# Cross-attention and mixture-of-experts kernel: the router's threshold search with one of its three counts on ScalarE, selection and slot positions rewritten, bf16 one-hots for the slots

## The reference

```python
T = B * S                                  # 2048 tokens
cap = max(1, T // E)                       # 256
probs = jax.nn.softmax(xt @ Wg, axis=-1)
pT = probs.T
_, top_idx = jax.lax.top_k(pT, cap)        # each expert takes its 256 likeliest tokens
sel = jnp.zeros((E, T), dtype=bool).at[jnp.arange(E)[:, None], top_idx].set(True)
masked = jnp.where(sel, pT, -jnp.inf)
assigned = sel.any(axis=0)
tok2exp = jnp.where(assigned, jnp.argmax(masked, axis=0), jnp.argmax(pT, axis=0))
...
h = jax.nn.gelu(xt @ W1[e], approximate=False) @ W2[e]     # weighted by the chosen probability
```

## Time and profile before

| | |
|---|---|
| device time, median of 3 | 428.44 us (428.04 to 429.25) |
| the profiled execution | 426.05 us, its span 424.2 us |
| busy: PE, ACT, DVE, POOL | 359.4, 259.4, 208.5, 118.9 us |
| router, from the last logits to the first index fetched by POOL | 279.5 to 326.6 us |
| mean granted TensorE clock | 0.93 of full speed |

### The profile page before, as it was taken

The page is one execution under the profiler, slowest core; times in us unless marked ns, Lnnn a source line. Parts: engine busy times, 40 slices in busy tenths (PEclk is TensorE's granted clock), DMA queues, the critical chain, the costliest instruction groups (busy, mean ns, idle before and its releaser), DMA issues.

```text
span 424.2 us, 10996 instructions
## 1 busy us (share of the span) xinstructions
PE 359.4 (85%) x4207; PEld 232.5 (55%) x4208; DVE 208.5 (49%) x785; ACT 259.4 (61%) x354; POOL 118.9 (28%) x175
## 2 busy tenths in 40 slices
PE   2989898999999999999999999841139799989893
PEld 1646456445343545453435468830039788879782
DVE  5849973745373646363646558358877010101010
ACT  1456456899999999999999925430000444444430
POOL 4244789300030303030302100000001345555543
PEclk9999999899999999999999999555559999999999
DMA  8325995304494446434842352800000322222210
GB/s 271 97 102 154 275 272 167 125 4 101 112 258 113 105 117 201 118 98 126 235 122 39 94 182 96 287 15 1 0 2 2 93 64 76 65 81 68 76 50 26
DMA packets 36760, 47.61 MB, mean 112 GB/s; under 512 B 8460, under 2 KB 25794, under 8 KB 36705
## 3 DMA queue, kind: packets, MB, share of 16 engines
q1 hardware_dynamic: 33808, 40.26, 33.2%
q0 software_dynamic: 2560, 6.30, 5.0%
q10 hardware_dynamic: 337, 0.32, 0.2%
HBM read 32.71 MB, written 13.81 MB: 110 GB/s over the span
## 4 chain that ended last, share of the span: by engine, by line
PE 63%; DVE 13%; ACT 9%; DMA 6%; issue 5%; SPq 2%; POOL 1%; POOLq 0%; ACTq 0%; DVEq 0%
PE ps L1002 15%; PE ps L981 14%; PE ps L966 7%; PE ps L1204 7%; PE ps L1194 7%; ACT pbuf L790 6%; PE ps L950 4%; DVE v_st L1581 3%; PE ps L1091 2%; PE ps L1065 2%; DMA pbuf<-in_L_xattn_Wkv 2%; DMA mid<-token_rows,take_ix 2%; DMA sums<-mid 2%; PE ps L1082 1%; SPq L491 1%
## 5 line engine op out<-in xcount | busy, mean ns | idle before, releaser
L790 ACT ACTIVATE pbuf<-ps 128x1024 f32<-128x1024 f32 (+3 forms) x192 | 169.3, 1030 | 3.6 <-PE ps L981 3.5
L1454 DVE SCALAR_TENSOR_TENSOR pbuf<-pbuf,seen 128x128 f32<-128x128 f32 (+2 forms) x288 | 79.2, 317 | 64.1 <-ACT pbuf L790 63.6
L981 PE MATMUL ps<-q_st,k_st 98*32 98x512 bf16 (+4 forms) x2048 | 102.5, 320 | 3.1 <-ACT pbuf L790 2.6
L1002 PE MATMUL ps<-pbuf,v_st 128*32 128x512 f32 (+4 forms) x1024 | 97.8, 477 | 1.0 <-DVE pbuf L1454 0.9
L981 PEld LDWEIGHTS ps<-q_st,k_st 98*32 98x32 bf16 x2048 | 52.5, 96 | 69.8 <-ACT pbuf L790 27.1
L667 POOL TENSOR_TENSOR mid<-mid 64x1024 f32<-64x1024 f32 x7 | 16.6, 2370 | 126.7 <-DMA mid<-reciprocals 109.3
L867 ACT COPY piece_f<-wts 128x1024 f32 x20 | 20.9, 1045 | 48.8 <-DVE more L1669 45.0
L1682 DVE SCALAR_TENSOR_TENSOR mid<-ps,slot_gate,mid 128x256 f32<-128x256 f32 x20 | 9.7, 484 | 81.9 <-PE ps L1204 81.9
L1204 PE MATMUL ps<-wts,mid 128*128 x160 | 39.0, 387 | 4.9 <-ACT mid L877 3.2
L1002 PEld LDWEIGHTS ps<-pbuf,v_st 128*32 128x32 f32 x1024 | 27.5, 110 | 25.7 <-issue 11.8
L1194 PE MATMUL ps<-mid,piece_f 128*128 128x128 f32 x320 | 39.1, 275 | 1.2 <-ACT mid L872 0.7
(11 more groups left out here) (215 smaller groups left out, 387.2 us busy)
## 6 DMA issues: line engine op xcount, KB each, us to landing
wts<-in_L_ffn_W SPq DMA_DIRECT2D x16, 512.0 KB, 4.9
k_st<-k_cut SPq DMA_DIRECT2D x48, 147.2 KB, 3.0
q_st<-q_cut SPq DMA_DIRECT2D x48, 128.0 KB, 2.9
q_cut<-wts SPq DMA_DIRECT2D x8, 384.0 KB, 3.6
k_cut<-wts SPq DMA_DIRECT2D x8, 384.0 KB, 4.2
xres<-in_x SPq DMA_DIRECT2D x4, 512.0 KB, 7.1
token_rows<-xres SPq DMA_DIRECT2D x4, 512.0 KB, 4.5
mid<-mid SPq DMA_DIRECT2D x28, 64.0 KB, 2.6
```

The costliest lines, as they stand in the source:

```text
L790: nc.scalar.activation(pbuf[:, s % 2, r, c0:c1], st_ps[(s * GH + r) % NST][:, c0:c1], ACT.Exp, scale=SCALE).then_inc(exp_done, 1)
L981: last = nc.tensor.matmul(st_ps[(s * GH + r) % NST][c:c + 32, a:z], k_st[pa][:, r, t * P + c:t * P + c + 32], q_st[pa][:, r, q0 + a - c0:q ...
L1002: last = nc.tensor.matmul(o_ps[32 * r:32 * r + 32, a:z], v_st[pa][:, t, r, :], pbuf[:, s % 2, r, a + dc:z + dc], start=(t == 0), stop=(t = ...
L1454: last = nc.vector.scalar_tensor_tensor(a, a, 3.0e38, seen[:, off:off + w], ALU.min, ALU.mult)
```

## The change

- **Keys.** They are fp32 in steps of 2 to the 15th, read by DVE straight from PSUM; the softmax is halved and stored expert-major. The second half's key comes from one instruction instead of four.
- **Rounds.** DVE makes two compares, ACT the third as `Sign(cand - key)` with a sum. PE adds a constant (a matmul that waits for nobody) and two products, one by `same_e` for DVE's counts, one by `same_h` (minus a half) for ACT's. `nxt` is now waited for.
- **Selection.** Sign, an equality, a scan, one combined order and one comparison; the way back is a bf16 matmul by `ident_2`. A bitwise or marks the held probability, a max-scan finds the peak, an equality makes the indicator `r_ind`.
- **Positions.** Offsets are made by matmuls (`same_s`, `prev_s`, `unbefore`, `lower_e`) and by adding a large constant that rounds to whole tiles.
- **Slots.** One-hots and operands are bf16. Token index first (32 matmuls), then the tiles' experts, then the weight in three bf16 parts (16 matmuls of 72 columns). The ring is gone. `keep_running` is 20, 40 and 20 in place of 80 and 90.
- Constants: `expert_constants` shrinks from 11 instructions to 1; `count_constants` (6 new) runs on DVE in the second group of heads.

```diff
@@ tensor
             for i in range(ROUNDS):
 
+                at = bank(1 + i % 2)[:, 0:3]
+                nc.tensor.matmul(at, ones_b[:, :], offset_b[:, 0:3], start=True, stop=False, skip_group_check=True)
                 pe.wait_ge(cnt_done, i + 1)
-                nc.tensor.matmul(bank(1)[:, 0:3], same_e[:, :], cnt_b[:, 0:3], start=True, stop=True).then_inc(tot_ready, 1)
+                nc.tensor.matmul(at[:, 0:2], same_e[:, :], cnt_d[:, 0:2], start=False, stop=True, skip_group_check=True)
+                pe.wait_ge(acnt_done, i + 1)
+                nc.tensor.matmul(at[:, 2:3], same_h[:, :], cnt_a[:, 0:1], start=False, stop=True,
+                                 skip_group_check=True).then_inc(tot_ready, 1)
...
-            keep_running(80)
...
+            keep_running(20)
+            pe.wait_ge(tile_v_done, 1)
             for t in range(TT):
                 pe.wait_ge(tile_made, t + 1)
-                last = nc.tensor.matmul(bank(3)[:, 0:2 * NS], in_tile[t % RING], hv[:, t, :, :].rearrange("p c n -> p (c n)"),
-                                        start=(t == 0), stop=(t == TT - 1)).then_inc(slots_ready, 1)
-
+                if t == 0:
+                    pe.wait_ge(row_v_done, 1)
+                nc.tensor.matmul(bank(3)[:, 0:NS], in_tile[t], tile_v[:, t, :], start=(t == 0), stop=False, skip_group_check=True)
+                last = nc.tensor.matmul(bank(3)[:, 0:NS], in_tile[t], row_v[:, t, :], start=False, stop=(t == TT - 1),
+                                        skip_group_check=True)
+            last.then_inc(slots_ready, 1)
+            keep_running(40)
+            pe.wait_ge(gate_v_done, 1)
+            for t in range(TT):
+                last = nc.tensor.matmul(bank(5)[:, 0:3 * NS], in_tile[t], gate_v[:, t, :, :].rearrange("p c n -> p (c n)"),
+                                        start=(t == 0), stop=(t == TT - 1))
+            last.then_inc(gates_ready, 1)
...
-            keep_running(90)
+            keep_running(20)
@@ scalar
-            nc.scalar.activation(warm[:, 3:4], ones_b[0:1, 0:1], ACT.Gelu)
+            nc.scalar.activation(warm[:, 3:4], ones_b[0:1, 0:1], ACT.Sign)
+
+            def compare(i):
+
+                act.wait_ge(cand_made, i + 1)
+                c = start_c[:, 0, :] if i == 0 else start_c[:, 1, :] if i == len(SHIFTS[0]) else cand
+                nc.scalar.activation(r_side, r_key[0 if i < len(SHIFTS[0]) else 1], ACT.Sign, scale=-1.0, bias=c[:, 3:4],
+                                     accum_out=cnt_a[:, 0:1]).then_inc(acnt_done, 1)
...
+            nc.scalar.activation(warm[:, 4:5], ones_b[0:1, 0:1], ACT.Gelu)
+            act.wait_ge(of_tile_done, 1)
+            nc.scalar.activation(row_v, of_tile, ACT.Identity, scale=frow[:, 0:1]).then_inc(row_v_done, 1)
@@ vector
-                    seq(nc.vector.scalar_tensor_tensor(r_eq, r_key[0], cand[:, 0:1], r_low, ALU.is_equal, ALU.mult))
-                    seq(nc.vector.tensor_scalar(r_sel, r_key[0], cand[:, 0:1], float((1 << LOW) + 1), ALU.is_gt, ALU.mult))
-                    seq(nc.vector.tensor_tensor(r_key[1], r_sel, r_eq, ALU.add))
-                    seq(nc.vector.tensor_scalar(cand[:, :], digit[:, i, :], 1.0, None, ALU.add))
-                for n, sh in enumerate(shifts):
-                    for j in range(1, 4):
-                        last = nc.vector.tensor_scalar(r_ge[j - 1], r_key[half], cand[:, j:j + 1], 0.0, ALU.is_ge, ALU.add,
-                                                       accum_out=cnt_b[:, j - 1:j])
+                    nc.vector.scalar_tensor_tensor(r_key[1], r_key[0], cand[:, 0:1], r_low, ALU.subtract, ALU.add).then_inc(cand_made, 1)
+                    v.wait_ge(cand_made, i + 1)
+                for n, w in enumerate(STEPS_OF[half]):
+                    for j in range(1, 3):
+                        last = nc.vector.tensor_scalar(r_junk[j], r_key[half], c[:, j:j + 1], 0.0, ALU.is_ge, ALU.add,
+                                                       accum_out=cnt_d[:, j - 1:j])
                     last.then_inc(cnt_done, 1)
...
+            nc.vector.tensor_scalar(r_eq, r_key[1], thr, 0.0, ALU.is_equal, ALU.add, accum_out=eq_n[:, 0:1]).then_inc(cnt_done, 1)
+            seq(nc.vector.tensor_tensor_scan(r_scan, r_one, r_eq, 0.0, ALU.mult, ALU.add))
+            v.wait_ge(acnt_done, ROUNDS + 1)
+            seq(nc.vector.scalar_tensor_tensor(r_order, r_side, APART, r_scan, ALU.mult, ALU.add))
...
+            nc.vector.tensor_scalar(r_sel, r_order, bank(5)[:, 0:1], float(CAP), ALU.add, ALU.is_le).then_inc(sel_done, 1)
...
+            seq(nc.vector.tensor_tensor(held3.bitcast(I32), bank(6)[:, 0:P].rearrange("p (e t) -> p t e", e=E).bitcast(I32), pr.bitcast(I32),
+                                        ALU.bitwise_or))
+            seq(nc.vector.tensor_tensor_scan(r_peak, r_keep, r_held, 0.0, ALU.mult, ALU.max))
+            nc.vector.tensor_tensor(r_ind3[:, 1:, :].rearrange("p e t -> p t e"), peak3,
+                                    peak3[:, :, E - 1:E].broadcast_to([P, TT, E]), ALU.is_equal).then_inc(ind_done, 1)
+            v.wait_ge(ind_done, 1)
+            seq(nc.vector.tensor_tensor(r_hot, r_ind[:, TT:], r_ind[:, 0:TE], ALU.subtract))
+            v.wait_ge(tot_there, 1)
+            nc.vector.tensor_copy(r_tot, bank(2)[:, 0:P]).then_inc(tot_done, 1)
+            v.wait_ge(tot_done, 1)
+            seq(nc.vector.tensor_scalar(r_gint, peak3[:, :, E - 1].bitcast(I32), (1 << 30) - 1, None, ALU.bitwise_and))
+            v.wait_ge(n_ready, 1)
+
+            seq(nc.vector.tensor_scalar(r_base, bank(0)[:, 0:1], P / 2 - 0.5, TO_TILES, ALU.add, ALU.add))
+            nc.vector.tensor_scalar(r_size, zeros_b[:, :], r_base, TO_TILES, ALU.add, ALU.subtract).then_inc(size_done, 1)
+            v.wait_ge(size_done, 1)
+            seq(nc.vector.tensor_scalar(r_nt, bank(0)[:, E:2 * E], P / 2 - 0.5, TO_TILES, ALU.add, ALU.add))
             v.wait_ge(rank_ready, 1)
+            seq(nc.vector.tensor_tensor(r_tmp, bank(1)[:, 0:TE], r_hot, ALU.mult))
+            seq(nc.vector.reduce_sum(r_pos, t3, AX.X))
+            seq(nc.vector.tensor_scalar(r_up, r_pos, -(P / 2 - 0.5), TO_TILES, ALU.add, ALU.add))
+            nc.vector.tensor_tensor(of_tile, r_up[:, :, None].broadcast_to([P, TT, NS]), r_mark[:, None, :].broadcast_to([P, TT, NS]),
+                                    ALU.is_equal).then_inc(of_tile_done, 1)
+            seq(nc.vector.scalar_tensor_tensor(r_lo, r_up, TO_TILES, r_pos, ALU.subtract, ALU.subtract))
+            v.wait_ge(of_tile_done, 1)
+            nc.vector.tensor_tensor(tile_v, of_tile, r_tilev[:, :, None].broadcast_to([P, TT, NS]), ALU.mult).then_inc(tile_v_done, 1)
+            for t in range(TT):
+                nc.vector.tensor_scalar(in_tile[t], fcol_n, r_lo[:, t:t + 1], None, ALU.is_equal).then_inc(tile_made, 1)
+
+            seq(nc.vector.tensor_scalar(r_nt, r_nt, TO_TILES, 1.0 / P, ALU.subtract, ALU.mult))
             seq(nc.vector.tensor_tensor_scan(r_end, r_one[:, 0:E], r_nt, 0.0, ALU.mult, ALU.add))
...
+            v.wait_ge(slots_ready, 1)
+            nc.vector.tensor_scalar(slot_tok[:, :], bank(3)[:, 0:NS], float(T), None, ALU.add).then_inc(idx_done, 1)
...
+            nc.vector.tensor_tensor(gate_v, of_tile[:, :, None, :].broadcast_to([P, TT, 3, NS]),
+                                    r_gs[:, :, :, None].broadcast_to([P, TT, 3, NS]), ALU.mult).then_inc(gate_v_done, 1)
...
```

More of the change, by code:

```diff
@@ L675, in _ @@
                 scale(g)
[L676 removed]
+            pool.wait_ge(idx_done, 1)
             pool.wait_ge(rows_sent, 16 * 2 * (TT // 4))
@@ L858, in _ @@
             act.sem_inc(fg_done, 2)
-            nc.scalar.activation(warm[:, 3:4], ones_b[0:1, 0:1], ACT.Gelu)
+            nc.scalar.activation(warm[:, 3:4], ones_b[0:1, 0:1], ACT.Sign)
[4 more added lines that the diff above has]
+                                     accum_out=cnt_a[:, 0:1]).then_inc(acnt_done, 1)
+            with nc.allow_low_precision(reason="counts of at most 128"):
+                for i in range(ROUNDS):
+                    compare(i)
+                act.wait_ge(cand_made, ROUNDS + 1)
+                nc.scalar.activation(r_side, r_key[1], ACT.Sign, scale=-1.0, bias=cand[:, 0:1],
+                                     accum_out=lt_n[:, 0:1]).then_inc(acnt_done, 1)
+            nc.scalar.activation(warm[:, 4:5], ones_b[0:1, 0:1], ACT.Gelu)
+            act.wait_ge(of_tile_done, 1)
+            nc.scalar.activation(row_v, of_tile, ACT.Identity, scale=frow[:, 0:1]).then_inc(row_v_done, 1)
             act.wait_ge(texp_done, 2)
@@ L1164, in _ @@
-            nc.tensor.matmul(bank(2)[:, 0:1], prev_e[:, :], cnt_b[:, 1:2], start=True, stop=True).then_inc(tot_ready, 1)
+            nc.tensor.matmul(at, same_h[:, :], eq_n[:, 0:1], start=False, stop=False, skip_group_check=True)
+            nc.tensor.matmul(at, prev_e[:, :], eq_n[:, 0:1], start=False, stop=True, skip_group_check=True).then_inc(tot_ready, 1)
             pe.wait_ge(sel_done, 1)
```

(31 more changed lines are left out.)

239 lines of the change are left out of this document (122 added, 117 removed).

## The result

The changed kernel takes **416.31 us** (median of 4 runs, 415.68 to 416.73), the kernel before 428.35 beside it (4 runs, 428.04 to 429.25): a ratio of 0.9714, 95% interval 0.9695 to 0.9734. In a second series it took 416.19 against 427.4 (5 runs, 413.37 to 416.25; ratio 0.972, 0.9689 to 0.9752). The prediction was 418.1, range 414.8 to 421.3, faster with a chance of 0.95.

What follows compares the result with a forecast made beforehand. The prediction took the router, one thread of short steps nearly all on DVE, as the bound. Savings of 11.65 us up to the token indices, less 1.3 given back, took 428.44 by -10.35 to 418.1 us; range 414.8 to 421.3.

Steps and rivals of the forecast that it cites:

- The forecast case: Whole kernel: ACT's count hidden, 11.65 us saved to the indices, 1.3 given back; 418.1 us, neighbours 416.9 to 419.6, chance 0.50.
- given back: Between token indices and first expert matmul: PE, its constants begun at the low clock, would be 1.3 us late.
- rival 2: Slots: the 16 bf16 one-hots run faster, 0.13 us apart in place of 0.22, 1.4 us less: 416.7; chance 0.16.
- keys, rounds, change of halves: Router's start: 15 rounds save 3.4 us, the first loses 0.1, change of halves saves 0.85, keys 0.2: 4.35.
- selection: Router after the rounds, up to its result on the token side: 1.90 us instead of 3.12, saves 1.22.
- expert: Finding each token's expert: bitwise or, scan and equality take 1.18 us instead of 3.73, saves 2.55.
- positions: Router step computing positions, by matmuls and short DVE steps: 2.72 us instead of 5.09, saves 2.37.
- slots, one-hots, tail: Router's end: slot operands save 0.43 us, the 16 one-hots stay at 3.54, the tail to the indices saves 0.73.
- `nxt`, now waited for, is done while PE works: Rounds: DVE's small step of 0.2 us fits beside PE's 0.05 to start and 0.20; round 1.34 us.
- Rival 1: Rounds: ACT ends last, its sum read in 0.4 us, 0.18 behind DVE; 15 rounds lose 2.7 us: 420.8; chance 0.12.
- Rival 4: Before the experts: clock up early, PE 0.1 us late in place of 1.3, projections give 0.3: 416.6; chance 0.12.
- Rival 3: Experts: clock stays low, a tile could cost 3 to 4 us more, eight end at about 445; chance 0.03.

## Why the prediction was right, and where its terms were off

The forecast case is nearest to what happened: ACT hidden, something given back behind the indices, the rest a plain sum. Part of rival 2 came with it. By its own terms, from the two chains (saved us, forecast and measured):

| part | forecast | measured | from |
|---|---|---|---|
| keys, rounds, change of halves | 4.35 | 3.10 | (304.66 - 279.33) against (307.92 - 279.49) |
| selection | 1.22 | 1.27 | 306.51 - 304.66 = 1.85 |
| expert | 2.55 | 2.12 | 308.12 - 306.51 = 1.61 |
| positions | 2.37 | 2.18 | 311.03 - 308.12 = 2.91 |
| slots, one-hots, tail | 1.16 | 2.23 | 315.45 - 311.03 = 4.42 against 6.65 |
| indices | 11.65 | 10.90 | |
| given back | 1.3 | 0.90 | 6.07 - 5.17 |

The logits ended 0.16 us earlier, the stretch from the first transpose to the end (92.38 against 92.53) took 0.15 less, and 0.07 less lay around the span: together 10.9 - 0.9 + 0.38 = 10.4. The agreement of the two profiled executions with the sum to 0.02 us is luck in good part: 0.75 less was saved than forecast, with single terms off by up to 1.25; 0.40 less was given back; and 0.38 came from stretches that the sum didn't hold. The forecast median, 418.1, was 1.8 above the measured one.

- **Rounds.** The step that failed is "`nxt`, now waited for, is done while PE works". It is done by then, but as a second wait ahead of the instruction that reads the totals it costs 0.08 us a round: 1.42 in place of 1.34. Shown by its removal, which gives 1.34 a round and takes 1.34 us off the router. ACT's compare saved the forecast amount: 0.24 a round by the run with it taken back (forecast 0.23). The change of halves saved its 0.85 exactly. At the keys 0.2 was forecast and 0.02 came (3.29 against 3.31 us from the logits to the first compare): three steps of the softmax became 0.07 to 0.08 us longer (0.38 in place of 0.30), where two at 0.06 were put, and the step that went was worth 0.26 rather than 0.33.
- **Rival 1** (ACT last) fell: the read-out of the sum takes 0.19 us, the upper bound, but begins 0.31 after the start of a Sign of 0.40.
- **Expert.** The equality was taken as a plain step of 0.32; it is 0.69, of which 0.31 are for its strided two-byte result. Shown by the contiguous form (0.39).
- **Positions.** 0.19 short; among it the sum over a strided view, 371 ns (L1727) where 0.29 was put. The rest is mostly the three places with two waits (L1716, L1721, L1726), 0.09 to 0.10 us behind a product in place of 0.02 to 0.04.
- **One-hots.** Kept at 3.54, measured 2.69: each 0.163 us behind the other in place of 0.22. This is rival 2, with six tenths of its size (0.85 of 1.4 us), and by the run with the fp32 column only 0.53 of it is the narrower input. The reason "the form with the operand gained nothing from its simplicity, and I keep 3.54" was wrong: the 59 ns between the rows of 286 and 227 were read as half the columns' time, but they may as well be a fixed price of the operand per partition, and nothing was known of a bf16 input.
- **Given back.** The mechanism (PE late because the 40 constants run at the low clock, which rises some 5 us behind their start) was seen in the profiled execution, with 5.6 us and 0.90 late. But it isn't a fixed price: with the rise 2.6 us behind the start the loss is 0.08, and the fetched rows come last. Rival 4's "clock up early" thus holds in most of the executions traced. Of the twelve traces of the changed kernel and its variants, seven have the rise 2.5 to 3.9 us behind the 40 constants' start and a gap of 5.18 to 5.27 us, five have it 4.3 to 5.6 us behind and a gap of 5.49 to 6.07. The rival's other half, a gain in the projections, did not show: PE has no wait for DVE there any more, and waits 0.94 us for ACT's copies, 0.35 before.
- **Rival 3** (an expert tile at the low clock) didn't come in any trace: from the first transposes on the granted clock is 1.00 in all those looked at, until the last tiles are done.

## What to carry to other kernels

In a thread of short steps between two engines, a second wait isn't free even if its condition is met before the other's: put the wait for the own result off, or let a later one cover it, and leave only the wait for the other engine ahead of the instruction that reads that engine's result (here 0.08 us of 1.42, 15 times). Moving one of several equal steps to an idle engine pays by what the chain loses less the second product (0.24 us), as long as the other engine's whole instruction and its read-out end first; that can be summed from rows of neighbouring forms. Where the result is narrow, write it contiguously and put the stride on the wide input (0.31 us in the one case measured). And compare kernels by stages measured between two of their own events, since the whole time held 2.4 us that had nothing to do with the edit.

## What the runs showed of the hardware that was not expected

- Two waits of DVE, first for an own result and then for a product of PE that ends last: the instruction behind them starts 0.09 to 0.12 us after the product's end, in place of 0.02 to 0.04 with one wait (L1680, L1716, L1721, L1726). Where the own result comes last (L1698, L1701) it starts 0.02 to 0.03 behind it.
- DVE, 128 columns, one operand per partition, a comparison: 286 ns from fp32 to fp32, 281 from fp32 to bf16, 249 from bf16 to bf16; back to back they start 0.198, 0.196 and 0.163 us apart.
- DVE, 128 fp32 pairs to bf16 with a comparison: 692 ns written with a stride of 16 elements, 386 ns written contiguously.
- ACT, 128 columns with a per-partition operand: 402 ns, and 189 ns to read out the sum, beginning 0.31 us after the start.
- The granted clock fell from 2.4 to 1.2 GHz with PE busy without a pause (at 265.0 us in the run with constants in the gap, at 265.6 before the change), and rose at one and the same place of the program 2.6 us behind the start of the 40 constants in one execution of the changed kernel and 5.6 in another.
